# One table in DRAM instead of two for the results of a mixture of experts, with one scatter at a time

## What is computed

```python
top = jnp.argmax(gate_logits, axis=-1)
h = jax.nn.gelu(jnp.einsum('bte,neh->nbth', x, W1) + b1[:, None, None, :], approximate=False)
y = jnp.einsum('nbth,nhe->nbte', h, W2) + b2[:, None, None, :]
out = jnp.einsum('nbte,btn->bte', y, onehot)
...
_, idx = jax.lax.top_k(score, K)
w = jax.nn.softmax(jnp.where(mask, score, -jnp.inf), axis=-1)
for e in range(E):
    mid = jax.nn.relu(jnp.einsum('bsd,fd->bsf', x, W1[e]) + b1[e])
    ye = jnp.einsum('bsf,df->bsd', mid, W2[e]) + b2[e]
    out = out + w[..., e:e + 1] * ye
```

## Time and profile before

| what | value |
|---|---|
| time, median of 3 runs | 1870.54 us (1867.48 to 1871.26) |
| profiled execution, span of its instructions | 1874.5 us |
| busy PE, PEld, DVE, ACT, POOL | 79%, 66%, 67%, 52%, 43% |
| chain that ended last: PE, DVE, DMA, POOL | 31%, 14%, 2%, 2% |
| scatters (L1396) | 68 of 96 KB |
| loads of results (L1358, L1359) | 24 of 384 KB |
| table fills (L1656) | 8 of 768 KB |
| predicated copies (L1366) | 12 |

### The profile page before, as it was taken

How to read it: one execution, slowest core, us unless ns; L and a number is a source line. 1 busy time by engine, 2 the same in 40 slices (tenths; PEclk the granted TensorE clock), 3 DMA queues, 4 the chain that set the end, 5 groups by cost and what they waited for, 6 DMA issues and landing times.

```text
span 1874.5 us, 42615 instructions
## 1 busy us (share of the span) xinstructions
PE 1483.1 (79%) x13098; PEld 1235.0 (66%) x13098; DVE 1247.8 (67%) x3542; ACT 977.2 (52%) x2392; POOL 808.0 (43%) x1177
## 2 busy tenths in 40 slices
PE   0589889798897997998988759759668887499992
PEld 0367678677676776776767648449646766389992
DVE  4788966788767888668896652433379896434344
ACT  0378733688434885348873223225348882155550
POOL 6577333684235762247733310124356521144440
PEclk9899989899899997999998968669869996599996
DMA  4666101743005550035610000147534511257765
GB/s 105 176 149 127 36 1 33 170 86 84 1 5 138 108 121 2 1 70 140 128 33 1 1 14 1 45 138 224 173 89 100 112 22 45 97 175 237 225 212 179
DMA packets 144317, 178.26 MB, mean 95 GB/s; under 512 B 22096, under 2 KB 106128, under 8 KB 143952
## 3 DMA queue, kind: packets, MB, share of 16 engines
q1 hardware_dynamic: 136784, 158.18, 32.9%
q0 software_dynamic: 7296, 17.18, 2.8%
HBM read 132.96 MB, written 42.34 MB: 94 GB/s over the span
## 4 chain that ended last, share of the span: by engine, by line
PE 31%; DVE 14%; issue 4%; DMA 2%; ACT 2%; POOL 2%; SPq 0%; DVEq 0%; POOLq 0%; ACTq 0%
PE bank L1473 7%; DVE ptl L799 4%; PE bank L1459 2%; DVE neg_max L792 2%; PE bank L645 1%; DVE xn L912 1%; PE bank L563 1%; PE bank L1460 1%; PE bank L1463 1%; PE bank L1461 1%; PE bank L1462 1%; PE bank L1217 1%; DMA xn<-y_rows 1%; PE bank L431 1%; PE bank L584 1%
## 5 line engine op out<-in xcount | busy, mean ns | idle before, releaser
L685 ACT ACTIVATE prob<-bank,neg_max 128x192 f32<-128x192 f32 (+1 forms) x960 | 406.9, 437 | 109.3 <-DVE neg_max L792 97.0
L792 DVE TENSOR_REDUCE neg_max<-bank 128x2 f32<-128x384 f32 (+1 forms) x480 | 274.3, 572 | 99.0 <-PE bank L544 91.4
L799 DVE TENSOR_TENSOR ptl<-bank,pth 128x384 f16<-128x384 f32 (+1 forms) x480 | 275.5, 574 | 4.6 <-ACT pth L698 4.0
L563 PE MATMUL bank<-ident,prob 128*128 128x128 f32 x1536 | 268.4, 288 | 0.0
L698 ACT ACTIVATE pth<-bank 128x384 f16<-128x384 f32 (+1 forms) x480 | 244.3, 509 | 9.3 <-PE bank L563 9.2
L652 ACT ACTIVATE xx<-bank 128x256 fp32r<-128x256 f32 x256 | 95.5, 386 | 196.0 <-PE bank L431 192.0
L544 PE MATMUL bank<-kx,qx 96*128 96x192 bf16 (+1 forms) x960 | 168.1, 257 | 1.1 <-DVE xx L766 1.1
L563 PEld LDWEIGHTS bank<-ident,prob 128*128 128x128 f32 x1536 | 162.9, 143 | 0.1
L584 PE MATMUL bank<-v,pth 128*128 128x33 bf16 x1152 | 138.4, 180 | 21.2 <-DVE ptl L799 18.0
L645 PE MATMUL bank<-w,fbuf 128*128 128x192 f32 x768 | 140.7, 327 | 2.0 <-DVE h L889 2.0
L734 ACT ACTIVATE fbuf<-bank,b 128x512 f32<-128x512 f32 x96 | 65.8, 687 | 146.5 <-PE bank L453 146.4
(11 more groups left out here) (295 smaller groups left out, 4522.5 us busy)
## 6 DMA issues: line engine op xcount, KB each, us to landing
xn<-in_e_seg SPq DMA_DIRECT2D x34, 768.0 KB
w<-in_e_w SPq DMA_DIRECT2D x23, 576.0 KB
qk_rows<-fbuf SPq DMA_DIRECT2D x128, 96.0 KB, 2.3
qx<-qk_rows SPq DMA_DIRECT2D x35, 288.0 KB, 4.0
kx<-qk_rows SPq DMA_DIRECT2D x35, 288.0 KB, 5.8
qk_rows<-w SPq DMA_DIRECT2D x80, 96.0 KB, 2.3
qx<-qk_rows SPq DMA_DIRECT2D x35, 192.0 KB, 4.6
kx<-qk_rows SPq DMA_DIRECT2D x35, 192.0 KB, 5.2
```

What stands on the lines that cost most here:

```text
L563: last = nc.tensor.transpose(bank[BT[p % 2]][:, c * P:c * P + P], probs_at(p, banded, c * P, P), ident[:, :])
L685: nc.scalar.activation(probs_at(p, banded, qt * n, n), scores_at(p, n)[:, qt, :], ACT.Exp, bias=neg_max[:, b % 2, hd, qt:qt + 1], scale=1. ...
L792: nc.vector.tensor_reduce(neg_max[:, b % 2, hd, :], scores_at(p, D if banded else S), AX.X, ALU.max, negate=True).then_inc(max_ready.sem, 1)
L799: nc.vector.tensor_tensor(ptl[:, p % 2, 0:n], bank[BT[p % 2]][:, 0:n], pth[:, p % 3, 0:n], ALU.subtract)\
```

## The change

There is one table and one semaphore. `sent(G, s)` is the count at which the scatters up to half `s` of tile `G` have landed. Every scatter waits for all scatters before it, the last one included, so never more than one is under way. `finish` waits for the same scatter as before. At a mixture's end there is one load per group and choice, none waits for a merge, and VectorE has neither the copies nor the predicate. The fills and the waits for them are gone: every row that is read has been scattered to. In the first mixture the wait between a group's addition and its statistics stands in the loop of the next group.

```diff
-        y_rows = [nc.dram_tensor(f"y_rows_{s}", ((2 * NT + 1) * P, D), F32, kind="Internal").ap() for s in range(2)]
+        y_rows = nc.dram_tensor("y_rows", ((2 * NT + 1) * P, D), F32, kind="Internal").ap()
...
+        def sent(G, s):
+
+            return 16 * (2 * G + s + 1)
+
         def sp_sums(sp, m):
 
-            y = [r[0:NT * P * PICKS[m], :].rearrange("(t p) d -> p t d", p=P) for r in y_rows]
-            for s in range(2):
-                sp.wait_ge(e_sent[s].sem, 16 * (span(m)[-1] + 1))
+            y = y_rows[0:NT * P * PICKS[m], :].rearrange("(t p) d -> p t d", p=P)
+            sp.wait_ge(e_sent.sem, sent(span(m)[-1], 1))
             for g in range(NG):
-                if g >= 2:
-                    sp.wait_ge(merged.sem, merged.at(m, g - 1))
                 for k in range(PICKS[m]):
                     tg, tk = slice(GT * g, GT * g + GT), slice(k * NT + GT * g, k * NT + GT * g + GT)
-                    sp.dma_start(sums(k)[:, tg, :], y[0][:, tk, :]).then_inc(sums_in[g].sem, 16)
-                    sp.dma_start(odd_sums(m, g, k), y[1][:, tk, :]).then_inc(sums_in[g].sem, 16)
-
-        def dve_merge(dve, ch, m, g):
-
-            dve.wait_ge(sums_in[g].sem, 32 * (PICKS[m] if m == 0 else PICKS[0] + PICKS[1]))
-            for k in range(PICKS[m]):
-                tg, tk = slice(GT * g, GT * g + GT), slice(k * NT + GT * g, k * NT + GT * g + GT)
-                ch.mark(nc.vector.copy_predicated(sums(k)[:, tg, :], d_odd[:, tk].unsqueeze(2).to_broadcast([P, GT, D]),
-                                                  odd_sums(m, g, k)))
-            ch.done(ch.n)
-            dve.sem_inc(merged.sem, 1)
+                    sp.dma_start(sums(k)[:, tg, :], y[:, tk, :]).then_inc(sums_in[g].sem, 16)
+
+        def dve_sums(dve, m, g):
+
+            dve.wait_ge(sums_in[g].sem, 16 * (PICKS[m] if m == 0 else PICKS[0] + PICKS[1]))
...
                 pool.wait_ge(e_y_ready.sem, 2 * G + s + 1)
-                if G > 0:
-                    pool.wait_ge(e_sent[s].sem, 16 * G)
+                if s or G > 0:
+                    pool.wait_ge(e_sent.sem, sent(G, s - 1))
                 i = 2 * (G - first) + s
-                pool.indirect_dma_start(out=y_rows[s], in_=vf[:, 2 * (G % 2) + s, :], in_offset=None,
+                pool.indirect_dma_start(out=y_rows, in_=vf[:, 2 * (G % 2) + s, :], in_offset=None,
                                         out_offset=bass.IndirectOffsetOnAxis(ap=put_at[:, i:i + 1], axis=0))\
-                    .then_inc(e_sent[s].sem, 16)
+                    .then_inc(e_sent.sem, 16)
...
                     if G >= 2:
-                        dve.wait_ge(e_sent[s].sem, 16 * (G - 1))
+                        dve.wait_ge(e_sent.sem, sent(G - 2, s))
...
-            ch.mark(v.tensor_scalar(d_odd[:, 0:b], d_pos_i[:, 0:b], P, None, ALU.bitwise_and))
...
-            sp.wait_ge(mask_ok.sem, 1)
-            filler = flat(mask[:, :, :], "p t d -> p (t d)").bitcast(F32).rearrange("p (t d) -> p t d", d=D)
-            for s in range(2):
-                for i in range(4):
-                    sp.dma_start(y_rows[s][8 * P * i:8 * P * (i + 1), :].rearrange("(t p) d -> p t d", p=P), filler)\
-                        .then_inc(filled.sem, 16)
...
-            sp.wait_ge(filled.sem, 16 * 8)
...
+            added = []
             for g in range(NG + 2):
                 if g < NG:
                     tg = slice(GT * g, GT * g + GT)
-                    dve_merge(dve, ch, 0, g)
-                    added = ch.mark(nc.vector.tensor_tensor(h[:, tg, 0:D], h[:, tg, 0:D], hb[:, tg, :], ALU.add))
+                    dve_sums(dve, 0, g)
+                    added.append(ch.mark(nc.vector.tensor_tensor(h[:, tg, 0:D], h[:, tg, 0:D], hb[:, tg, :], ALU.add)))
+                if g:
+                    ch.done(added[min(g, NG) - 1])
                 if g == NG:
-                    ch.done(added)
                     dve.sem_inc(sum_ready.sem, 1)
...
-                dve_merge(dve, ch, 1, g)
+                dve_sums(dve, 1, g)
```

More of the change, by code:

```diff
@@ L232, in build_tower @@
         d_mul = part(128)
-        d_pos, d_div, d_pos_i, d_mod, d_odd = part(32), part(32), part(32, I32), part(32, I32), part(32, I32)
+        d_pos, d_div, d_pos_i, d_mod = part(32), part(32), part(32, I32), part(32, I32)
         d_many, d_more = part(8), part(64, dims="p (e j) -> p e j", e=8)
@@ L334, in build_tower @@
         e_b2_in = [sig(f"e_b2_in_{j}", base=0) for j in range(3)]
-        e_sent = [sig(f"e_sent_{s}", base=0) for s in range(2)]
-        merged = sig("merged", per=NG, base=0)
-        filled = sig("filled", base=0)
+        e_sent = sig("e_sent", base=0)
         e_turned = sig("e_turned", base=0)
@@ L1311, in build_tower @@
                           .rearrange("p (t d) -> p t d", d=D))[k]
-        odd_sums = lambda m, g, k: spare[:, NT * 256 + ((2 * (g % 2) + k) - 4 if m else g % 2 - 2) * GT * D:][:, 0:GT * D]\
-            .rearrange("p (t d) -> p t d", d=D)
         marks = lambda m: chosen[:, 0:(NT + 1) * EXPERTS[m]].rearrange("p (t e) -> p t e", e=EXPERTS[m])
```

## The result

| | median of the runs | against the kernel before |
|---|---|---|
| before | 1870.9 us (1867.48 to 1871.35) | |
| the change | 1924.84 us (1915.77 to 1928.33) | 1.0293 (95% interval 1.0269 to 1.0317) |

A forecast was written before the change was run, and what follows sets the result against it. It took the chain of waits as spread thin, with savings counting where it passes the two expert stages' ends. 11.5 + 4.6 + 0.2 = 16.3 us off the profiled span, shifted to the runs' median, gave 1854.3 us, range 1851 to 1862.

The forecast's parts named there:

- The serial scatters inside a stage: Expert stages: each scatter waiting for the one before to land fits into a tile's 8.63 us; cost nothing.
- come once per tile in a burst: Expert stages: the weights' loads slow only one of a tile's two scatters, so two landings stay under 8.63 us.
- 2.33 + 5 or 6: Expert stages: mean of a tile's two landings, one quiet, one beside loads, in us; claimed to fit 8.63 us.
- covers of 13.7 and 17.3 us: Expert stages: time from a gather to its use, and until a scatter's buffer is rewritten; said to absorb late tiles.
- The first rival: POOL's wait before every scatter: scatters bound the expert stages, 71 us, about 1925 us, from 9.2 us per tile; chance 0.06.
- The second stage's end: After the second stage's last scatter: fewer loads and no copies save 12.6 us, net 11.5 us (10 to 12.5).
- The serial last scatter: Last scatter of each expert stage: waits for the one before and lands about 1.1 us later.
- The first stage's end: After the first stage's last scatter: group 3's addition starts 5.8 us earlier, net 4.6 us less (4 to 5.2).
- The fills and the bit tests: Table fills at the start are hidden, gain 0; two bit tests in the chain's serial part save 0.2 us together.

The follow-up runs named there:

- Experiment 2: The change, and the kernel before as control, each with a sixth of each expert's weights loaded: 1851.73 us and 1863.32 us.
- experiment 3: The change with gathers between a tile's scatters and two tiles further ahead, with eight result buffers, and with both: 1921.79, 1924.9 and 1920.88 us.
- with sixths: The change with each expert's second weight matrix in six loads and each segment of the first in four: 1882.4 us.

## Why the prediction was wrong

**The step that failed** is "The serial scatters inside a stage", costed at nothing. It cost 59 us in the profiled executions (16.6 + 42.4), on 10 and 22 tiles that each became 1.6 and 1.9 us longer. Three parts of its argument were wrong.

- *The weights' loads "come once per tile in a burst, so that only one of the two scatters can meet it."* The burst is about as long as the tile. In the change's second stage, the two rows of SP that load weights in one tile, and the median landing of each kind there, in us:

```profile
1690.04 0.33 SPq L1339 DMA_DIRECT2D w<-in_e_w  x1
...
1691.98 0.34 SPq L1330 DMA_DIRECT2D xn<-in_e_seg  x1
```

```profile
xn<-in_e_seg SPq DMA_DIRECT2D x19, 768.0 KB, 6.4
w<-in_e_w SPq DMA_DIRECT2D x13, 576.0 KB, 4.0
```

  By these medians some load is on its way from 1690.04 to about 1698.4 (1691.98 + 6.4), an estimate of 8.3 us for a tile that took 8.27 before. In the window of the kernel before the DMA engines are busy 67% of the stage. Both scatters of a tile can be late: those issued at 1693.63 and 1700.17 landed 5.76 and 6.79 us later. Experiment 2 shows what the loads are worth.
- *The tile was summed from two landings alone.* From one scatter to the next it takes 3.08 us even when no weights are loaded (1897.27 to 1900.35), against a landing of 2.33. So each awaited scatter costs about 0.75 us more than its landing, 1.5 us per tile, and the sum of "2.33 + 5 or 6" becomes 8.8 to 9.8 instead of 7.3 to 8.3 us. (The 8.66 us of the earlier trace rows are from scatter to scatter and hold this step already; the 2.33 do not.) Behind a tile's second scatter the two gathers come first, so that even after a quiet landing the next scatter goes out 3.85 us later and not 3.08 (1715.38 to 1719.23, landing 2.34).
- *A tile of 8.63 us, and covers of 13.7 and 17.3 us.* Most tiles took about 8.6 us, but the mean was 8.27. TensorE was busy 98% of the stage, so there was no slack in TensorE either. The covers did not help, and longer ones would not have (experiment 3). That POOL waited only 3.0 us before was no evidence: it waited for a scatter a whole tile old.

**The first rival came true**, with 1925 us beside a measured 1924.84. Its place and its rule are shown: the pace rose over 9.2 us per tile, and POOL waits where it said. Its picture of a quiet and a busy landing in turn is not: the distances behind a tile's first and second scatter are alike (5.32 and 4.77 us), not some 3 and 8.7. That the number fits is partly luck. It put 2.4 us on 30 tiles, 71 us; the profile has 1.6 and 1.9 us on 32 tiles, 59 us, and 7.9 us at the start that no other profile has in full. Its chance of 0.06 rested on the three errors above.

**The second stage's end held.** SP's first load to VectorE's end is 17.18 us (1902.70 to 1919.88) where 16.4 was forecast and 28.98 stood before: -11.8 against -12.6. The first data came after 4.59 us (forecast 4.44); the rest of the missing 0.8 us is the second group, which waited 0.91 us for its loads. The serial last scatter cost 1.8 us (3.08 in place of 1.27), not 1.1, for the 0.75 us above. Net 10 us, the lower bound given.

**The first stage's end held.** Group 1's addition starts 4.49 us after SP's first load (forecast 4.44) and group 3's 12.0 us after it (forecast 11.85 to 12.5, before 18.0). With 1.8 us off for the last scatter the 6.0 us are 4.2 net, inside the 4 to 5.2 given. (The forecast's 5.8 less 1.1 is 4.7, not 4.6, which changes nothing.)

**The fills and the bit tests** cost nothing that shows: from profile to profile the first gather moves more than their 0.2 us.

## What to carry to other kernels

A wait for a transfer inside a loop is costed at the loop's rate: add up everything that now follows one after the other in one turn, with the landings as they are beside the loop's own traffic and the time from landing to the next issue, and compare with the pace of the bounding engine. Buffers and early gathers help against a single late transfer and not against a sum that is too long in every turn. That an old wait hardly ever bound says nothing about a new wait for the same transfer one step earlier; one awaited landing per turn was free here once the waiting queue had other work to do in it, and the second one was not.

## What was not expected of the hardware

- With the quiet landing of 2.33 us, the last scatter had landed at 1902.68 (1900.35 + 2.33), and SP's load starts at 1902.70, 0.02 us later. POOL's next scatter starts 0.75 us after the landing of the one before it: the last four pairs of the second stage are each 3.08 us apart (1888.03 to 1900.35), with landings of 2.33 us. Beside loads it was 0.78 us (1693.63 + 5.76 to 1700.17).
- Cutting loads of 768 and 576 KB into pieces of 192 and 96 KB left the median distance of the waiting scatters (4.34 and 4.36 us) and took away nearly all over 6 us (21 of 66 in the change, 3 with sixths).
- In the second stage TensorE's mean granted clock was 1.00 (2.4 GHz) before and 0.93 after, and the same matrix products were busy 188.36 us instead of 179.35. The 0.93 holds stretches at the lower level: from 1718 to 1721 us TensorE was busy 0.00 of 3 us, and from 1721 to 1727 us the clock was 0.50 (1.2 GHz). So in this stage a TensorE that waited was also slower; in the version with one wait and moved gathers, with TensorE busy 176.09 of 179.50 us, the clock was 1.00.
